# Cross-attention: the row maximum enters the transposed scores by a 16-row product of its own

## What is computed

```python
scores = jnp.einsum('bhqd,bhkd->bhqk', qh, kh) / jnp.sqrt(jnp.asarray(hd, jnp.float32))
m = mask[:, None, None, :]
scores = jnp.where(m, -jnp.inf, scores)
w = jax.nn.softmax(scores, axis=-1)
w = jnp.where(m, 0.0, w)
out = jnp.einsum('bhqk,bhkd->bhqd', w, vh)
```

## Time and profile before

| | |
|---|---|
| median of 3 runs | 725.49 us (724.27 to 726.21) |
| the profiled execution, span | 767.7 us |
| TensorE busy | 613.9 us, 80% |
| VectorE busy | 557.7 us, 73% |
| ScalarE busy | 476.2 us, 62% |
| GpSimd busy | 479.1 us, 62% |
| mean granted clock of TensorE | 0.918 |

### The profile page before, as it was taken

The page is one execution under the profiler, slowest core; times in us unless marked ns, Lnnn a source line. Parts: engine busy times, 40 slices in busy tenths (PEclk is TensorE's granted clock), DMA queues, the critical chain, the costliest instruction groups (busy, mean ns, idle before and its releaser), DMA issues.

```text
span 767.7 us, 19357 instructions
## 1 busy us (share of the span) xinstructions
PE 613.9 (80%) x6308; PEld 528.3 (69%) x6308; DVE 557.7 (73%) x1699; ACT 476.2 (62%) x975; POOL 479.1 (62%) x655
## 2 busy tenths in 40 slices
PE   2578999999897779999999999987877889888300
PEld 0367887788896568888888878876755677777300
DVE  4998999999955676878878787955546355567665
ACT  4675888888745567777676767754242344457434
POOL 6277877778863555446777776835347445467753
PEclk9699999999999599999999999999978799999855
DMA  6611211212234334433110100002211222351141
GB/s 181 191 17 19 26 22 24 24 24 22 37 81 151 136 127 150 175 138 134 35 34 18 30 18 25 18 24 61 58 60 58 81 71 67 98 160 52 49 137 55
DMA packets 113107, 55.39 MB, mean 72 GB/s; under 512 B 70625, under 2 KB 103841, under 8 KB 113025
## 3 DMA queue, kind: packets, MB, share of 16 engines
q1 hardware_dynamic: 103984, 25.46, 15.0%
q10 hardware_dynamic: 4496, 19.02, 6.3%
q0 software_dynamic: 4544, 9.84, 3.7%
HBM read 21.25 MB, written 33.05 MB: 71 GB/s over the span
## 4 chain that ended last, share of the span: by engine, by line
PE 53%; DVE 15%; issue 12%; ACT 10%; another core or an unknown queue 3%; POOL 3%; DMA 3%; SPq 1%; ACTq 0%; DVEq 0%; POOLq 0%
PE PS L1194 14%; PE PS L991 10%; PE PS L1102 5%; PE PS L1112 4%; DVE PS L1911 3%; PE PS L1302 2%; PE PS L1161 2%; PE PS L1283 2%; PE PS L1300 2%; PE PS L1285 1%; PE PS L1301 1%; DMA W_raw<-in_L_ffn_W_dram 1%; DVE W_raw L2287 1%; PE PS L1284 1%
## 5 line engine op out<-in xcount | busy, mean ns | idle before, releaser
L991 PE MATMUL PS<-prod,ident 128*128 128x144 f32 x1024 | 137.1, 294 | 8.7 <-DVE hctx L1891 8.4
L991 PEld LDWEIGHTS PS<-prod,ident 128*128 128x128 f32 x1024 | 131.4, 195 | 16.5 <-issue 9.3
L1194 PE MATMUL PS<-W_raw 128*72 128x128 f32 x1024 | 131.0, 284 | 8.5 <-issue 4.5
L760 POOL TENSOR_TENSOR prod<-prod,v 128x2048 f32<-128x2048 f32 x32 | 117.5, 3673 | 31.0 <-ACT prod L1397 31.0
L1194 PEld LDWEIGHTS PS<-W_raw 128*72 128x72 f32 x1024 | 117.3, 149 | 14.0 <-issue 7.5
L880 POOL DMA_INDIRECT ys<-W_raw,ids x78 | 77.3, 991 | 63.5 <-ACT W_raw L1635 40.4
L2174 DVE TENSOR_REDUCE m<-PS 128x8 f32<-128x1024 f32 x64 | 77.9, 1218 | 43.5 <-PE PS L1112 43.5
L2287 DVE SCALAR_TENSOR_TENSOR W_raw<-PS,W_raw 128x512 f16<-128x512 f32 x78 | 52.1, 688 | 66.4 <-ACT W_raw L1619 35.4
L820 POOL DMA_INDIRECT xs<-Y,spot_u x64 | 64.3, 1005 | 26.4 <-issue 15.0
L1911 DVE TENSOR_REDUCE PS<-pair_sq 128x128 f32<-128x1024 f32 x64 | 75.0, 1218 | 0.0
L1553 ACT ACTIVATE W_raw<-PS 128x1024 f32<-128x1024 f32 x64 | 65.8, 1028 | 14.1 <-remote 10.7
(11 more groups left out here) (321 smaller groups left out, 1548.5 us busy)
## 6 DMA issues: line engine op xcount, KB each, us to landing
xs<-pad ACTq DMA_DIRECT2D x16, 1152.0 KB, 4.5
Y<-xs SPq DMA_DIRECT2D x39, 144.0 KB
W_raw<-ys SPq DMA_DIRECT2D x16, 256.0 KB
W_raw<-in_L_ffn_W_dram SPq DMA_DIRECT2D x1, 2048.0 KB
shuffle<-hctx SPq DMA_DIRECT2D x32, 64.0 KB, 3.0
Y<-shuffle SPq DMA_DIRECT2D x32, 64.0 KB, 1.8
cs<-in_ctx_dram SPq DMA_DIRECT2D x8, 256.0 KB
out_dram<-W_raw SPq DMA_DIRECT2D x8, 256.0 KB, 2.9
```

Source lines behind the costliest of these rows:

```text
L760: pool.tensor_tensor(rows[:, :, 0:D].rearrange("p t (d h) -> p t d h", d=HD), a.broadcast_to((P, H, HD, H)), v.broadcast_to((P, H, HD, H)) ...
L991: last = pe.matmul(PS[:, 6, 0:TC], ident[:], prod2[:, i % 2, TC * t:TC * (t + 1)], start=(t == 0), stop=(t == H - 1))
L1194: last = pe.matmul(PS[0:HO, 7, a * P:(a + 1) * P], v_frame[:, i % 2, a, HO * n:HO * (n + 1)], PT[:, i % 2, 8 * a + n, :], start=(n == 0), ...
```

## The change

The second turning of the query rows goes. `QT` gets four buffers instead of two, so that the turned queries are still there for the transposed scores. The maximum is cut into two 16-bit parts by two steps instead of five and written into an array of its own, `m_parts`: 64 columns for the even heads and 64 for the odd ones, of which 16 each (8 heads, two parts) are used. One turning of 128x128 brings it onto rows 0 to 15 and 64 to 79 (`mT`). In the transposed scores each pair of products has 49 rows a head and is followed by a pair of 16 rows that adds the maximum: its fixed operand `minus_rows` holds -1 in the two rows of its head and 0 in the others. `m_parts`, `mT` and `minus_rows` take the place of stage A's `w_pairs`, and GpSimd writes them in `prepare_pads`.

```diff
-        QT, QmT, KT = QKT[:, 0:2], QKT[:, 2:4], QKT[:, 4:8]
+        QT, KT = QKT[:, 0:4], QKT[:, 4:8]
+        MR = 2 * HG
+        minus_rows = w_pairs[:, 0:HG * P].rearrange("p (g k) -> p g k", g=HG)
+        m_parts, mT = (w_pairs[:, (HG + n) * P:(HG + n + 2) * P].rearrange("p (b q) -> p b q", b=2) for n in (0, 2))
...
+        def max_part(b, part):
+            return m_parts[:, b].rearrange("p (r x) -> p r x", r=HR)[:, :, part:MR:2].rearrange("p r g -> p g r")
...
                 ch(pool.memset(QK[:, :, 0, :, 6 * HD], 1.0))
-                pool.memset(QK[:, :, 1, :, 6 * HD + 1:6 * HD + 4], 1.0).then_inc(pads_ready, 1)
+                ch(pool.memset(m_parts, 0.0))
+                own = minus_ident[:].rearrange("p (r x) -> p r x", r=HR)
+                ch(pool.tensor_tensor(minus_part[:], own[:, :, 0:MR:2], own[:, :, 1:MR:2], ALU.add))
+                ch.settle()
+                ch(pool.tensor_tensor(minus_head[:], minus_part[:, 0], minus_part[:, 1], ALU.add))
+                ch.settle()
+                pool.tensor_tensor(minus_rows, bc(minus_head[:], P), ones[:].unsqueeze(1).broadcast_to((P, HG, P)),
+                                   ALU.mult).then_inc(pads_ready, 1)
...
-                def half_scores(a, left, right, used, ready):
+                def half_scores(a, left, right, ready, largest=None):
+                    used = 6 * HD + 1
                     for g in range(HG // 2):
                         for r in range(HR):
                             rows = slice(HS * r, HS * r + used)
                             last = pe.matmul(PS[:, 2 * a + r, g * P:(g + 1) * P], left[rows, HG // 2 * a + g, :],
-                                             right[rows, HG // 2 * a + g, :], start=True, stop=True)
+                                             right[rows, HG // 2 * a + g, :], start=True, stop=largest is None)
+                        if largest is not None:
+                            for r in range(HR):
+                                rows = slice(HS * r, HS * r + MR)
+                                last = pe.matmul(PS[:, 2 * a + r, g * P:(g + 1) * P], minus_rows[rows, HG // 2 * a + g, :],
+                                                 largest[rows, :], start=False, stop=True)
...
-                    spread(4, i, 0, qmT_psum)
+                    pe.transpose(PS[:, 4, 0:P // 2].bitcast(BF16), m_parts[:, i % 2, :], ident16[:]).then_inc(qmT_psum, 1)
...
+                        if u == 1 and j == 1:
+                            after(pe, pads_ready, 1)
-                        half_scores(a, KT[:, i], QmT[:, i % 2], 6 * HD + 4, scoreT_psum)
+                        half_scores(a, KT[:, i], QT[:, i], scoreT_psum, mT[:, i % 2, :])
...
-                    act.copy(QmT[:, i % 2].rearrange("p a d -> p (a d)"), PS[:, 4, :].bitcast(BF16)
-                             ).then_inc(qmT_ready, 1)
+                    act.copy(mT[:, i % 2, :], PS[:, 4, 0:P // 2].bitcast(BF16)).then_inc(qmT_ready, 1)
...
-                    after(act, score_psum, 2 * (k - 2))
-                    act.copy(QT[:, i % 2].rearrange("p a d -> p (a d)"), PS[:, 4, :].bitcast(BF16)
+                    after(act, scoreT_psum, 2 * (k - 4))
+                    act.copy(QT[:, i].rearrange("p a d -> p (a d)"), PS[:, 4, :].bitcast(BF16)
...
+                        after(dve, m_ready, k - 2)
                         after(dve, score_psum, 2 * (k - 2) + a + 1)
...
                     after(dve, max_done, 2 * (k - 1))
-                    parts3 = QK[:, i, 0, :, 6 * HD + 1:6 * HD + 4]
-                    step(dve.tensor_scalar(m_neg[:], m2[:], -1.0, -0.1 * NEG, ALU.mult, ALU.min))
...
-                    dve.tensor_tensor(parts3[:, :, 2], m_rest[:, 0], parts3[:, :, 1], ALU.subtract
-                                      ).then_inc(m_ready, 1)
+                    after(dve, qmT_psum, k - 3)
+                    m = m2[:].rearrange("p (g r) -> p g r", r=HR)
+                    high = max_part(i % 2, 0)
+                    step(dve.tensor_scalar(high, m, 0.1 * NEG, None, ALU.max))
+                    settle()
+                    dve.scalar_tensor_tensor(max_part(i % 2, 1), m, 0.1 * NEG, high, ALU.max, ALU.subtract
+                                             ).then_inc(m_ready, 1)
```

More of the change, by code:

```diff
@@ L272, in decoder_layer @@
         outT = frames[0:HO, 4 * VF:4 * VF + 2 * P]
-        QT, QmT, KT = QKT[:, 0:2], QKT[:, 2:4], QKT[:, 4:8]
+        QT, KT = QKT[:, 0:4], QKT[:, 4:8]
         m2 = sb("m2", [P, H])
-        m_neg = sb("m_neg", [P, H])
-        m_rest = sb("m_rest", [P, 1, H])
+        MR = 2 * HG
+        minus_rows = w_pairs[:, 0:HG * P].rearrange("p (g k) -> p g k", g=HG)
+        m_parts, mT = (w_pairs[:, (HG + n) * P:(HG + n + 2) * P].rearrange("p (b q) -> p b q", b=2) for n in (0, 2))
+        minus_part = sb("minus_part", [P, HR, HG])
+        minus_head = sb("minus_head", [P, HG])
         PT = W1_raw[:].rearrange("p (a h) q -> p a h q", a=2)
@@ L1140, in b_slot @@
                         after(pe, max_done, 2 * (k - 3) + a + 1)
-                        half_scores(a, QT[:, i % 2], KT[:, i], 6 * HD + 1, score_psum)
+                        half_scores(a, QT[:, i], KT[:, i], score_psum)
                 l, i = divmod(j - 1, TB)
@@ L2208, in b_slot @@
                     after(dve, max_done, 2 * (k - 1))
-                    parts3 = QK[:, i, 0, :, 6 * HD + 1:6 * HD + 4]
-                    step(dve.tensor_scalar(m_neg[:], m2[:], -1.0, -0.1 * NEG, ALU.mult, ALU.min))
+                    after(dve, qmT_psum, k - 3)
+                    m = m2[:].rearrange("p (g r) -> p g r", r=HR)
+                    high = max_part(i % 2, 0)
+                    step(dve.tensor_scalar(high, m, 0.1 * NEG, None, ALU.max))
                     settle()
-                    step(dve.tensor_copy(parts3[:, :, 0], m_neg[:]))
-                    settle()
-                    step(dve.tensor_tensor(m_rest[:, 0], m_neg[:], parts3[:, :, 0], ALU.subtract))
-                    settle()
-                    step(dve.tensor_copy(parts3[:, :, 1], m_rest[:, 0]))
-                    settle()
-                    dve.tensor_tensor(parts3[:, :, 2], m_rest[:, 0], parts3[:, :, 1], ALU.subtract
-                                      ).then_inc(m_ready, 1)
+                    dve.scalar_tensor_tensor(max_part(i % 2, 1), m, 0.1 * NEG, high, ALU.max, ALU.subtract
+                                             ).then_inc(m_ready, 1)
                 if there(2) and u != T + 1:
```

## The result

The changed kernel takes **769.08 us** (768.47 to 772.84, 4 runs), the kernel before, timed beside it on the same chip, 725.85 us (724.27 to 727.15): a ratio of 1.0613, 95% interval 1.0585 to 1.0641, or +43.2 us. The forecast was 758, range 738 to 774: slower, as forecast, and within the range, but 10 us more than forecast.

What follows compares the result with a forecast made beforehand. TensorE's time in the steady cross-attention was taken as the bound: +45 us on TensorE, -11 from filled waits, +34 in the profile, taken as +33 on the 725.5 us median, giving 758 us; range 738 to 774.

Steps and rivals of the forecast that it cites:

- What bounds the kernel: Steady cross-attention, 283 to 500 us: TensorE busy 206.7 of 217.0 us, so its added time arrives nearly whole.
- A step's price: TensorE, transposed scores: a pair costs 0.06 us, each change of array height some 0.09 more; +1.80 us a batch.
- The second turning, ScalarE, VectorE: Per batch: seven turnings fewer, -0.39 us on TensorE; ScalarE's copy -0.76 and VectorE's chain -0.7, both off the path.
- What TensorE's waits give back: Longer products fill existing TensorE waits: 5 us before L1194, 1.5 before L1167, 4.5 outside the steady stage; together -11 us.
- The way from the profile to the median: Profiled execution 5.8% longer than the runs; if evenly stretched, +34 us becomes 32, and +33 was taken.
- GpSimd once: One-time setup of constants on GpSimd: +2.1 us of work, priced at 0, or 0.8 once if uncovered.
- Rival A: Changes between 64 and 32 rows free, freed VectorE and ScalarE time removes 9.8 us of TensorE waits: 717.5 us; 7%.
- rival B: Changes between 64 and 32 rows free, but TensorE's waits stay: 727 us, the same; 5%.
- Rival C: The two 16-row products of a pair do not overlap: 14 us more, so 772 us; 6%.
- Rival D: Only one direction of height change costs: 18 to 24 us less, so 738 to 745 us; 5%.

Runs made afterwards that it cites:

- base_look: The kernel before, with no edit, profiled a second time; 725.99 us, profiled span 724.2 us.
- high64: The changed kernel with the maximum's product on 49 rows a head instead of 16, the height of the scores; 730.01 us, ratio 1.0058.
- early16: The changed kernel, TensorE turning the next query rows before half_outputs(0) and ScalarE copying the turned maximum before its two casts; 767.41 us, ratio 1.0590.
- half1: The changed kernel with the maximum's product on 16 rows only in the second half of the heads, 49 in the first; 749.10 us, ratio 1.0319.

## Why the prediction was right, and where it was off

**What bounds the kernel: right.** TensorE's time in the cross-attention decided; the stage grew by 42.2 us and the span by 42.5. A slot takes 38.06/4 = 9.5 us, forecast 9.4, and TensorE is idle for 1.3 us of the stretch, forecast under 10.3. From the first shifted product to the last it took 300.6 us against 255.9 in `base_look`: "some 30 us longer" was too little. It is 35 against the first profile, which was the longer one, and the next points have the rest.

**A step's price: right in kind, a tenth too small.** "Each change of the height that the array is split into costs some 0.09 us beyond the ordinary step", and it was used as a step of 0.15. The change between 64 and 32, which no row of before showed, costs as the others do and a little more than the upper bound that was taken; the measured steps are 0.16, so 0.105 beyond the step. A half grew by 1.44 - 0.48 = 0.96 us instead of 0.90, and TensorE's sum is 32 x (2 x 0.96 - 0.39) = +49 us instead of +45.

**The second turning, ScalarE, VectorE: right.** -0.39 us a batch on TensorE; copy 0.26 us forecast 0.25; chain 0.46 forecast 0.5; off the path, as their idle time shows.

**What TensorE's waits give back: off, by 2 to 3 us.** -11 us was forecast. 49 - 42.2 = 6.8 came, and 1.65 of the 42.2 is the lower clock in one tile, so the waits gave 8.4. In the steady stage all of them filled, as forecast: a tile of `base_look` loses 0.38 us before L1194 and 0.54 before L1167, and 4 x 1.53 - 0.92 = 5.20 us more a tile is what comes (measured 38.06 - 32.93 = 5.13). Over 217 us that is 6.1, and 5 + 1.5 = 6.5 was forecast, but by luck: "13 such waits, 6.6 us ... I take 5 us" before L1194 was read from the execution that was 42 us too long and is 2.5 in the undisturbed one, and the 1.5 before L1167 is 3.6. The term that was off is the 4.5 us outside the steady stage; some 2.3 are left for it.

**The way from the profile to the median: off, by 1 to 2 us.** "If the stretch is even, 34 becomes 32. I take +33." The stretch lay mostly in the experts, so nothing was to be taken off.

**Together**: +4 for the step, +2.6 for the waits, +1.7 for the lower clock in one tile, +1 for the stretch, from 33 to 42, against 43.2 measured. All of them lie on one side. The lower clock was no term of the sum; the forecast named it as a way to be wrong upwards, and the profiled execution has it once in the steady stage.

**GpSimd once, priced at 0: right.** The first score product comes 0.9 us later in the profile after (249.8 against 248.9), but so does the first turning of rows for the projections (L1085 before, L1099 after; 214.0 against 213.1), which lies some 11 us ahead of the new constants; from there to the first score product it is 35.8 us in both profiles of before and in the one after.

**Rival A** (free changes, and the freed time of VectorE and ScalarE pays 9.8 us) fell twice: the changes aren't free, and in `high64`, where they are avoided, the freed time alone pays nothing. `high64` is rival B's case, and came out 3 us above its 727, since the removed turnings lay ahead of a wait. **Rival C** fell by the trace, though its 772 is nearer to 769 than the forecast's 758: the two 16-row products of a pair start within 0.01 us of each other, like the others. **Rival D** fell: a step takes 0.16 in both directions.

**What stays open:** why the granted clock fell for 3.4 us in the middle of the stage (`early16`, with the same products, has 37.97 or 37.98 us in all four steady tiles), and what disturbed the first profile of before.

## What to carry to other kernels

Before an operation is made smaller on TensorE, write down the heights of the products in the order in which they run: each change costs twice an ordinary small product, and padding with zeros to the neighbours' height (here 49 rows for 16) was worth 39 of 43 us. A saving has to be placed against the wait that follows it: seven turnings saved ahead of a wait brought nothing, until later work was moved into the gap, and that move paid only once the small copy that it needed stood early on its own engine, too (733.5 with one of the two, 718.6 with both). And when a profile's span does not fit the runs, a second profile comes before any sum of waits: in the disturbed execution of this case the steps were those of the others, the waits were not. The granted clock by windows belongs to that reading; it explains a tile that is too long and has no wait.

## What the runs showed of the hardware that was not expected

A change of the array's height costs much the same beyond an ordinary step whether it goes between 64 and 32 rows (0.10 to 0.11 us) or in from 128 and out again (0.09 to 0.105), and as much where TensorE has waits (`half1`) as where it has none (`early16`). A pair of products that adds to what stands in its bank costs 0.056 us on 49 rows, like a pair that starts one; right behind a change of height it is 0.066, on 49 rows and on 16. Two executions of one kernel differed by 31 us in the experts, with a granted clock of 0.78 against 0.98 over 50 us of them, and by nothing in TensorE's steps in the cross-attention. And in the changed kernel the granted clock fell to 0.50 for 3.4 us in a tile in which TensorE had hardly been idle; it cost 1.65 us.
